# Interference stage of a tower kernel: a Newton step for all four lengths, half of the folding on VectorE, the third sum begun ahead of a negation

## The chip, the cores and the metric

One of the eight NeuronCores of a Trainium2 chip. The metric is the device time of one execution in microseconds (us), taken as the median of several executions. The profile shows one execution of its own; it is read against that execution's own time. Engines: TensorE (PE, with PEld for its weight loads), VectorE (DVE), ScalarE (ACT), GpSimd (POOL) and the SyncE queue (SP), which here issues most of the transfers.

## The reference, cut to what matters

1024 tokens pass two encoders and an attention over four states. What follows is the stage that this case is about. `R` and `I` are real and imaginary parts of four states `n` of 512 values for each token.

```python
R = einsum('bnd,ned->bne', attn_r, int_Wr) - einsum('bnd,ned->bne', attn_i, int_Wi)
I = einsum('bnd,ned->bne', attn_r, int_Wi) + einsum('bnd,ned->bne', attn_i, int_Wr)
phase = arctan2(I_i * R_j - R_i * I_j, R_i * R_j + I_i * I_j)     # for every pair i, j of states
f = cos(phase) * strength[..., None]
sup_r = einsum('bijd,bjd->bd', f, R)
sup_i = einsum('bijd,bjd->bd', f, I)
norm = sqrt(sum(sup_r ** 2 + sup_i ** 2) + 1e-08)
```

Then `sup / norm` goes through the measuring matrices, an amplitude, a layer norm, a GELU and three top layers (the tail). The kernel never forms a phase: the cosine of a phase between two states is the dot product of their unit vectors, so it needs `1 / sqrt(R^2 + I^2)` for each of the four states, and that length again to weigh the states in the sum.

## The kernel before, in words

All of it stands in `phase_states`. The tokens are eight tiles `t` of 128. The program of every engine is written out by hand and runs in its own order; engines meet in semaphores only. Tiles 0, 1 and 7 (LAST) are written out on VectorE and 2 to 6 are a hardware loop; on ScalarE the loop holds tiles 1 to 6.

For one tile:

- **PE** (`vectors(t, n)`, L52 to L54): 48 matmuls of 128x512 for each state `n`, results in banks `2n` (real) and `2n+1` (imaginary). It may overwrite the banks of state `n` once the unit vector of the tile before has been read out of them (`unit`). Its left operands `s_axng` are loaded into two buffers by SP (`load`, L787), and ScalarE makes the negated copies (`negate`, L994).
- **ACT**: `squares(t, n)` (L1003, L1004) puts the squares of both banks into `sqr` and `sqi`, which have two slots, shared by states 0/2 and 1/3. `magnitude` makes a mask `zero` (L1012) and the length `mag` (L1013, Sqrt). `seed` (L1017) overwrites `sqi` with a first guess of 1/length for states 2 and 3. `begin(t, 0, j)` (L1032) starts the weights `inv` from the dot product `p` that VectorE has just made. `length` and `scale` (L1042 to L1048) normalise the folded sum of the tile before. Functions of different tables need an ACT_TABLE_LOAD between them.
- **DVE** (class `Tile`): `add_squares(t, n)` (L1423) for states 0 and 1, written into the middle and the end of the tile before; `invert(n)` (L1333), a hardware reciprocal of 128x512 for states 0 and 1; `unit_vector(n)` (L1350); `add_23` (L1337); `pair(0, 1)` (L1355 to L1363); `refine` (L1341, L1343), one Newton step from the guess, for states 2 and 3 together; unit vectors 2 and 3; then the pairs 02, 03, 12, 13, 23, each four instructions with one or two `weigh` (L1372) and some `rescale` (L1378); last `product` (L1417), 128x4096, which multiplies all four vectors by their weights.
- **POOL** (`fold`, L872, L875): adds vectors 0 to 2 and 1 to 3 (two instructions of 128x1024), then 2 to 3 into `sup`. Beside it stands, on VectorE, the next tile's work.

ScalarE's order in a tile is squares 0, magnitude 0, negate(t, 3), squares 1, magnitude 1, negate(t+1, 0), squares 2 and 3, magnitude 2 and 3, seed, negate(t+1, 1), begin 1 (twice), length, begin 2, negate(t+1, 2), scale, begin 3. In the last tile it also splits weight pieces into high and low parts (`pieces`, L956; on VectorE L1284) and works for the tail (`sup_high`, L1078; on VectorE `sup_low`, L1451, L1453).

Of the kernel before, what the change touches and what calls it, by code (L numbers as in the profile page):

```python
# [10 lines left out]
ALU = mybir.AluOpType  # L11
# [512 lines left out]
def phase_states(nc, g):  # L524
# [13 lines left out]
    STEPS = 2 + 1 + 6 + 2 * 6 + 3 + sum(WEIGHED.values())  # L538
    W_MR, W_MI, W_POST, W_T1, W_T2 = 0, KD, 2 * KD, 3 * KD, 4 * KD
    with s.ctx:  # L540
# [327 lines left out]
        def _(pool):  # L868
            def fold(t):
                pool.wait_ge(weighed, t + 1)  # L870
                for n in range(2):
                    pool.tensor_tensor(cs[:, :, n + 2, :], cs[:, :, n, :], cs[:, :, n + 2, :], ALU.add).then_inc(folded, 1)  # L872
                pool.wait_ge(folded, t * 3 + 2)
                pool.wait_ge(stored, t * 16)
                pool.tensor_tensor(sup[:, :, :], cs[:, :, 2, :], cs[:, :, 3, :], ALU.add).then_inc(folded, 1)  # L875
# [11 lines left out]
            with pool.Fori(1, TT) as t:  # L887
                fold(t)

        @block.scalar  # L890
        def _(act):
# [114 lines left out]
            def magnitude(t, n0, n1):  # L1006
                n = slice(n0, n1)
                m = slice(n0 % 2, n0 % 2 + n1 - n0)
                act.wait_ge(summed, t * 3 + (min(n0, 2) + 1))
                if not zeroth(t):  # L1010
                    act.wait_ge(rescaled, t * 3 - (2 - min(n0, 2)))
                act.activation(zero[:, n, :], sqi[:, m, :], ACT.Relu, scale=-1.0 / LEAST, bias=k01[:, 1:2])  # L1012
                act.activation(mag[:, n, :], sqi[:, m, :], ACT.Sqrt, bias=k01[:, 0:1]).then_inc(mag_done, 1)  # L1013

            def seed(t):
                act.wait_ge(mag_done, t * 3 + 3)
                act.activation(sqi[:, :, :], sqi[:, :, :], ACT.Abs_reciprocal_sqrt, bias=k01[:, 0:1]).then_inc(seeded, 1)  # L1017
# [32 lines left out]
            def body(t, first):  # L1050
                squares(t, 0)
                magnitude(t, 0, 1)
                negate(t, 3)
                squares(t, 1)
                magnitude(t, 1, 2)
# [3 lines left out]
                magnitude(t, 2, 4)  # L1059
                seed(t)  # L1060
# [39 lines left out]
            def gelu(t):  # L1100
# [3 lines left out]
                else:  # L1104
                    act.wait_ge(newton, TT)
# [47 lines left out]
            magnitude(t, 0, 1)  # L1153
            negate(t, 3)
            squares(t, 1)
            magnitude(t, 1, 2)
# [5 lines left out]
            magnitude(t, 2, 4)  # L1162
            seed(t)
# [35 lines left out]
        def _(dve):  # L1199
# [119 lines left out]
            class Tile:  # L1319
# [9 lines left out]
                def invert(self, n):  # L1329
                    dve.wait_ge(mag_done, self.t * 3 + (n + 1))  # L1330
                    if not self.first and n == 0:
                        dve.wait_ge(weighed, self.t)
                    self.link(dve.reciprocal(inv[:, n, :], mag[:, n, :]))  # L1333

                def add_23(self):
                    dve.wait_ge(squared, self.t * 8 + 8)
                    dve.tensor_tensor(sqi[:, :, :], sqr[:, :, :], sqi[:, :, :], ALU.add).then_inc(summed, 1)  # L1337

                def refine(self):
                    dve.wait_ge(seeded, self.t + 1)  # L1340
                    self.link(dve.scalar_tensor_tensor(out=sqr[:, :, :], in0=mag[:, 2:4, :], scalar=-1.0, in1=sqi[:, :, :],  # L1341
                                                       op0=ALU.mult, op1=ALU.mult))
# [10 lines left out]
                def pair(self, i, j):  # L1353
                    t, p = self.t, p_of(i, j)
# [596 lines left out]
```

## Time and profile before

| what | us |
|---|---|
| median of 3 executions | 3120.39 (3120.31 to 3123.47) |
| the profiled execution, whole | 3116.82 |
| its span, first to last instruction | 3115.2 |
| first unit-vector work on VectorE of this stage to the end of tile 6 | 2559.1 to 2914.4 |
| last tile with the head of the tail | 2914.4 to about 2979 |
| the rest of the tail | about 2979 to 3115.2 |

How to read the profile: a timeline row gives the start in us, the duration, the engine, the line of the kernel, output<-input, and in brackets the idle time ahead of it with what ended it. Instructions of one engine overlap a little (the next starts some 0.08 us before the end shown), so that steps on a path are counted from start to start. The granted clock PEclk is a share of 2.4 GHz; 0.5 is the other level, 1.2 GHz.

### The profile page before, as it was taken

What the parts mean: (1) busy time and instruction counts of PE and PEld (TensorE: products, weight loads), DVE (VectorE), ACT (ScalarE), POOL (GpSimd) and SP (SyncE); (2) the same over time, 40 slices, a digit from 0 to 9 for tenths busy, and PEclk for the clock granted to TensorE, in tenths of its full rate; (3) what the DMA queues carried; (4) which work ended last, traced back from release to release, by engine and by line L of the source; (5) the groups of instructions that cost most, each with busy time, mean ns of one, the idle gap of its engine ahead of it and who ended that gap; (6) DMA issues with size and microseconds to landing.
All of it is one profiled execution on the core that took longest, in us unless ns stands there. A gap on an engine that the chain in (4) does not pass through costs nothing. (4 is left out here: it accounts for less than half of the span.)

```text
span 3115.2 us, 43855 instructions
## 1 busy us (share of the span) xinstructions
PE 2981.3 (96%) x15808; PEld 2582.6 (83%) x15808; DVE 1571.7 (50%) x2819; ACT 1111.3 (36%) x1873; POOL 233.0 (7%) x241
## 2 busy tenths in 40 slices
PE   8999999999699999999979999999999989999798
PEld 7888888888588877888879999999999977777686
DVE  3222222212531125221257767667667659999973
ACT  3111111111331114211235555545555554454553
POOL 1000000000110111110000000000000001212100
PEclk9999999999899999999989999999999999999899
DMA  5222222221442334332432232231231373433410
GB/s 203 75 77 74 74 77 74 64 60 61 152 146 77 101 98 139 106 104 76 152 120 55 69 93 54 80 81 54 84 78 54 101 183 81 108 94 88 147 40 11
DMA packets 364353, 285.48 MB, mean 92 GB/s; under 512 B 280193, under 2 KB 280321, under 8 KB 364161
## 3 DMA queue, kind: packets, MB, share of 16 engines
q1 hardware_dynamic: 341632, 206.97, 23.6%
q0 software_dynamic: 22656, 77.67, 7.2%
q8 instruction: 38, 0.62, 0.1%
q14 instruction: 27, 0.21, 0.0%
HBM read 194.40 MB, written 90.18 MB: 91 GB/s over the span
## 5 line engine op out<-in xcount | busy, mean ns | idle before, releaser
L52 PE MATMUL banks<-a_whi,g_hi 128*128 128x512 f32 x1152 | 449.0, 390 | 9.6 <-DVE a_wlo L185 9.6
L53 PE MATMUL banks<-a_wlo,g_hi 128*128 128x512 f32 x1152 | 448.8, 390 | 0.0
L54 PE MATMUL banks<-a_whi,g_lo 128*128 128x512 f32 x1152 | 448.6, 389 | 0.0
L52 PE MATMUL banks<-g_hi,b_whi 128*128 128x512 f32 x1024 | 400.6, 391 | 1.2 <-issue 1.2
L53 PE MATMUL banks<-g_lo,b_whi 128*128 128x512 f32 x1024 | 399.0, 390 | 0.0
L54 PE MATMUL banks<-g_hi,b_wlo 128*128 128x512 f32 x1024 | 398.8, 389 | 0.0
L185 DVE TENSOR_TENSOR a_wlo<-a_wraw,a_whi 128x512 fp32r<-128x512 f32 x144 | 99.6, 692 | 569.2 <-ACT a_whi L171 569.2
L171 ACT ACTIVATE a_whi<-a_wraw 128x512 fp32r<-128x512 f32 x144 | 91.0, 632 | 660.2 <-PE banks L54 660.2
L52 PE MATMUL banks<-t_sx,g_hi 128*128 128x256 f32 x1024 | 294.2, 287 | 17.7 <-DMA t_sx<-s_scr 17.7
L396 DVE TENSOR_TENSOR b_wlo<-b_wraw,b_whi 128x512 fp32r<-128x512 f32 x128 | 88.2, 690 | 433.3 <-ACT b_whi L341 433.1
L53 PE MATMUL banks<-t_sx,g_hi 128*128 128x256 f32 x1024 | 291.0, 284 | 0.0
L54 PE MATMUL banks<-t_sx,g_lo 128*128 128x256 f32 x1024 | 290.9, 284 | 0.0
L1206 DVE TENSOR_SCALAR t_ks<-banks,cols 64x256 f32<-64x256 f32 x512 | 236.5, 482 | 80.5 <-PE banks L54 73.3
L52 PEld LDWEIGHTS banks<-a_whi,g_hi 128*128 128x128 f32 x1152 | 216.6, 188 | 54.6 <-issue 9.5
L53 PEld LDWEIGHTS banks<-a_wlo,g_hi 128*128 128x128 f32 x1152 | 216.7, 188 | 45.1
L54 PEld LDWEIGHTS banks<-a_whi,g_lo 128*128 128x128 f32 x1152 | 216.6, 188 | 44.9
L341 ACT ACTIVATE b_whi<-b_wraw 128x512 fp32r<-128x512 f32 x128 | 80.3, 629 | 446.8 <-PE banks L54 446.1
L52 PE MATMUL banks<-g_hi,s_axng 128*128 128x512 f32 x512 | 205.6, 402 | 26.0 <-DVE s_cs L1350 23.4
L52 PEld LDWEIGHTS banks<-g_hi,b_whi 128*128 128x128 f32 x1024 | 192.7, 188 | 40.6 <-issue 1.4
L54 PEld LDWEIGHTS banks<-g_hi,b_wlo 128*128 128x128 f32 x1024 | 192.7, 188 | 40.3
L53 PEld LDWEIGHTS banks<-g_lo,b_whi 128*128 128x128 f32 x1024 | 192.7, 188 | 39.8
L52 PEld LDWEIGHTS banks<-t_sx,g_hi 128*128 128x128 f32 x1024 | 197.9, 193 | 18.4 <-issue 14.6
(158 smaller groups left out, 5567.0 us busy)
## 6 DMA issues: line engine op xcount, KB each, us to landing
a_wraw<-w_first SPq DMA_DIRECT2D x144, 256.0 KB, 2.6
b_wraw<-w_second SPq DMA_DIRECT2D x128, 256.0 KB, 2.6
t_sx<-s_scr SPq DMA_DIRECT2D x64, 512.0 KB, 4.1
a_scr<-t_at SPq DMA_DIRECT2D x256, 128.0 KB, 1.9
s_axng<-a_scr SPq DMA_DIRECT2D x64, 512.0 KB, 5.3
g_wraw<-w_pieces SPq DMA_DIRECT2D x82, 256.0 KB, 4.5
h_scr<-a_hst POOLq DMA_DIRECT2D x72, 256.0 KB, 2.7
b_hl<-h_scr POOLq DMA_DIRECT2D x16, 1024.0 KB, 5.9
```

Source lines behind the costliest of these rows:

```text
L52: mm(out, ahi, bhi, start=first, stop=False)
L53: mm(out, ahi, blo, start=False, stop=False)
L54: return mm(out, alo, bhi, start=False, stop=last)
L171: act.activation(whi[:, k % SPL, :], wraw[:, k % RAW, :], ACT.Copy).then_inc(w_hi, 1)
L185: dve.tensor_tensor(wlo[:, k % SPL, :], wraw[:, k % RAW, :], whi[:, k % SPL, :].bitcast(F32), ALU.subtract).then_inc(w_split, 1)
L341: act.activation(whi[:, j % SPL, :, :].rearrange("p a n -> p (a n)"), wraw[:, j % RAW, :], ACT.Copy).then_inc(w_hi, 1)
L396: dve.tensor_tensor(wlo[:, j % SPL, :, :].rearrange("p a n -> p (a n)"), wraw[:, j % RAW, :], whi[:, j % SPL, :, :].bitcast(F32).rearrange ...
L1206: ins = dve.tensor_scalar(ks[half(at_half), m % 2, h, part, :], b_k[half(h), m % 2, e * C:(e + 1) * C], bcol(M_K + e, m, half(h)), float(s ...
```

## The change

Four edits, all in this stage:

1. `invert` goes. All four lengths take the guess and Newton step: `lengths(t, h)` on ScalarE for the states of half `h` (0 and 1, or 2 and 3) computes the guess into `sqr`, then the length, then the mask; `refine(h)` on VectorE does the two instructions into `inv`.
2. Since the guess of half 0 now lies in `sqr`, `squares(t, 2)` and `squares(t, 3)` wait for `refine(0)`. The two half-size sums of squares become one of 128x1024, `add_squares(0)` just ahead of `product`; `add_23` becomes `add_squares(1)` and stands behind both unit vectors 0 and 1.
3. The two POOL additions into vectors 2 and 3 become one VectorE addition of 128x2048 behind `product`. POOL keeps the last addition, and waits for `refine(0)` of the next tile before it starts.
4. On ScalarE `negate(t+1, 2)` moves from ahead of `scale` and the third `begin` to behind them.

```diff
@@ POOL, fold
             def fold(t):
-                pool.wait_ge(weighed, t + 1)
-                for n in range(2):
-                    pool.tensor_tensor(cs[:, :, n + 2, :], cs[:, :, n, :], cs[:, :, n + 2, :], ALU.add).then_inc(folded, 1)
-                pool.wait_ge(folded, t * 3 + 2)
+                pool.wait_ge(folded, t * 2 + 1)
+                if not isinstance(t, int) or t < LAST:
+                    pool.wait_ge(newton, t * 2 + 3)
                 pool.wait_ge(stored, t * 16)
                 pool.tensor_tensor(sup[:, :, :], cs[:, :, 2, :], cs[:, :, 3, :], ALU.add).then_inc(folded, 1)
@@ ACT
             def squares(t, n):
                 act.wait_ge(multiplied, t * 8 + (2 * n + 2))
                 if n >= 2:
-                    act.wait_ge(mag_done, t * 3 + (n - 1))
+                    act.wait_ge(mag_done, t * 4 + 2)
+                    act.wait_ge(newton, t * 2 + 1)
                 elif not zeroth(t):
-                    act.wait_ge(newton, t)
+                    act.wait_ge(mag_done, t * 4)
+                    act.wait_ge(newton, t * 2)
...
-            def magnitude(t, n0, n1):
...
-            def seed(t):
...
+            def lengths(t, h):
+                n = slice(2 * h, 2 * h + 2)
+                act.wait_ge(summed, t * 2 + (h + 1))
+                act.activation(sqr[:, :, :], sqi[:, :, :], ACT.Abs_reciprocal_sqrt, bias=k01[:, 0:1]).then_inc(seeded, 1)
                 if not zeroth(t):
+                    act.wait_ge(rescaled, t * 3 - (1 - h))
+                act.activation(mag[:, n, :], sqi[:, :, :], ACT.Sqrt, bias=k01[:, 0:1]).then_inc(mag_done, 1)
+                act.activation(zero[:, n, :], sqi[:, :, :], ACT.Relu, scale=-1.0 / LEAST, bias=k01[:, 1:2]).then_inc(mag_done, 1)
...
             def body(t, first):
                 squares(t, 0)
-                magnitude(t, 0, 1)
                 negate(t, 3)
                 squares(t, 1)
-                magnitude(t, 1, 2)
+                lengths(t, 0)
                 negate(t + 1, 0)
                 squares(t, 2)
                 squares(t, 3)
-                magnitude(t, 2, 4)
-                seed(t)
+                lengths(t, 1)
...
                 begin(t, 0, 2)
-                negate(t + 1, 2)
                 if not first:
                     scale(t - 1)
                 begin(t, 0, 3)
+                negate(t + 1, 2)
@@ DVE, class Tile
+                def refine(self, h):
+                    n = slice(2 * h, 2 * h + 2)
+                    dve.wait_ge(seeded, self.t * 2 + (h + 1))
+                    dve.wait_ge(mag_done, self.t * 4 + (2 * h + 1))
...
+                    self.link(dve.scalar_tensor_tensor(out=inv[:, n, :], in0=mag[:, n, :], scalar=-1.0, in1=sqr[:, :, :],
                                                        op0=ALU.mult, op1=ALU.mult))
...
+                    dve.scalar_tensor_tensor(out=inv[:, n, :], in0=inv[:, n, :], scalar=2.0, in1=sqr[:, :, :],
                                              op0=ALU.add, op1=ALU.mult).then_inc(newton, 1)
...
                 def units(self):
-                    self.invert(0)
+                    self.refine(0)
                     self.unit_vector(0)
-                    self.add_23()
-                    self.invert(1)
                     self.unit_vector(1)
+                    self.add_squares(1)
...
                                       ALU.mult).then_inc(weighed, 1)
+                    dve.wait_ge(weighed, self.t + 1)
+                    dve.tensor_tensor(cs[:, :, 2:4, :], cs[:, :, 0:2, :], cs[:, :, 2:4, :], ALU.add).then_inc(folded, 1)
...
                 tile.pairs_12()
-                add_squares(t + 1, 0)
                 tile.pairs_13()
                 tile.pairs_23()
-                add_squares(t + 1, 1)
+                Tile(t + 1, False).add_squares(0)
                 tile.product()
```

Where this moves instructions, in the steady loop. REGISTER_ALU and ISA rows are small steps of the sequencer that compute a semaphore value. First VectorE, the head of a tile (loop of tiles 2 to 6); before:

```order
L1333 RECIPROCAL s_inv<-s_mag 128x512 [waits s_weighed,s_mag_done]
L1327 ISA
L1349 REGISTER_ALU [waits s_chain]
L1350 TENSOR_TENSOR s_cs<-banks,s_inv 128x2x512 [waits s_folded]
L1336 ISA
L1337 TENSOR_TENSOR s_sqi<-s_sqr,s_sqi 128x1024 [waits s_squared]
L1330 REGISTER_ALU
L1333 RECIPROCAL s_inv<-s_mag 128x512 [waits s_mag_done]
L1327 REGISTER_ALU
L1349 REGISTER_ALU [waits s_chain]
L1350 TENSOR_TENSOR s_cs<-banks,s_inv 128x2x512 [waits s_folded]
L1355 TENSOR_TENSOR s_zz<-s_zero 128x512
```

and with the change:

```order
L1331 ISA [waits s_seeded]
L1334 SCALAR_TENSOR_TENSOR s_inv<-s_mag,s_sqr 128x1024 [waits s_weighed,s_mag_done]
L1322 ISA
L1336 SCALAR_TENSOR_TENSOR s_inv<-s_inv,s_sqr 128x1024 [waits s_chain]
L1342 REGISTER_ALU [waits s_newton]
L1343 TENSOR_TENSOR s_cs<-banks,s_inv 128x2x512 [waits s_folded]
L1343 TENSOR_TENSOR s_cs<-banks,s_inv 128x2x512
L1325 ISA
L1326 TENSOR_TENSOR s_sqi<-s_sqr,s_sqi 128x1024 [waits s_squared]
L1349 REGISTER_ALU
L1350 TENSOR_TENSOR s_zz<-s_zero 128x512 [waits s_mag_done]
```

Two reciprocals have given way to two Newton instructions of double width, and the sum of squares of states 2 and 3 has moved from between the unit vectors to behind them.

Second ScalarE, from the squares of state 2 to the copy of the strengths; before:

```order
L1003 ACTIVATE s_sqr<-banks 128x512 [waits s_mag_done,s_multiplied]
L1004 ACTIVATE s_sqi<-banks 128x512
L998 REGISTER_ALU
L1003 ACTIVATE s_sqr<-banks 128x512 [waits s_mag_done,s_multiplied]
L1004 ACTIVATE s_sqi<-banks 128x512
L1009 REGISTER_ALU
L1012 ACTIVATE s_zero<-s_sqi,g_k 128x1024 [waits s_rescaled,s_summed]
L1013 ACTIVATE s_mag<-s_sqi,g_k 128x1024
L1017 ACT_TABLE_LOAD
L1017 ACTIVATE s_sqi<-s_sqi,g_k 128x1024 [waits s_mag_done]
```

and with the change:

```order
L1005 ACTIVATE s_sqr<-banks 128x512 [waits s_newton,s_mag_done]
L1006 ACTIVATE s_sqi<-banks 128x512
L998 REGISTER_ALU
L1005 ACTIVATE s_sqr<-banks 128x512 [waits s_newton,s_mag_done,s_multiplied]
L1006 ACTIVATE s_sqi<-banks 128x512
L1010 REGISTER_ALU
L1011 ACT_TABLE_LOAD
L1011 ACTIVATE s_sqr<-s_sqi,g_k 128x1024 [waits s_summed]
L1014 ACT_TABLE_LOAD
L1014 ACTIVATE s_mag<-s_sqi,g_k 128x1024 [waits s_rescaled]
L1015 ACTIVATE s_zero<-s_sqi,g_k 128x1024
```

The guess comes first, with a table load ahead of the instruction that waits for the sum, a second table load follows it, and the squares wait for VectorE's Newton step.

Third GpSimd, its loop over the tiles; before:

```order
L872 TENSOR_TENSOR s_cs<-s_cs 128x2x512 [waits s_weighed]
L872 TENSOR_TENSOR s_cs<-s_cs 128x2x512
L873 ISA
L874 REGISTER_ALU [waits s_folded]
L875 TENSOR_TENSOR s_sup<-s_cs 128x1024 [waits s_stored]
L887 REGISTER_ALU
```

and with the change:

```order
L872 REGISTER_ALU [waits s_folded]
L873 REGISTER_ALU [waits s_newton]
L874 TENSOR_TENSOR s_sup<-s_cs 128x1024 [waits s_stored]
L886 REGISTER_ALU
L886 COMPARE_AND_BRANCH
```

One of three additions is left on GpSimd, behind a wait for the next tile's Newton step.

## Rows read from the trace of the kernel before

**Rows 1.** By stretch: busy us (count) of PE, PEld, DVE, ACT, POOL; PEclk; DMA share; GB/s.
```profile
2700.00:2750.00 50.00, 45.94 (x192) 37.48 (x191) 47.56 (x50) 25.51 (x37) 7.93 (x3) 0.93 0.39 94
...
2622.00:2628.00 6.00, 5.43 (x13) 4.32 (x14) 5.96 (x4) 4.30 (x4) 3.80 (x2) 0.52 0.05 11
```

**Rows 2.** PE in order of time: the first matmul of tile 2's product.
```profile
2622.57 0.80 PE L52 MATMUL banks<-g_hi,s_axng 128*128 128x512 f32 x1 [6.16 <-DVE s_cs L1350]
```

**Rows 3.** VectorE in order of time, tile 2, from its start to the next.
```profile
2666.92 3.35 DVE L1333 RECIPROCAL s_inv<-s_mag 128x512 f32<-128x512 f32 x1
...
2677.28 0.41 DVE L1355 TENSOR_TENSOR s_zz<-s_zero 128x512 bf16<-128x512 bf16 x1
...
2680.70 1.22 DVE L1341 SCALAR_TENSOR_TENSOR s_sqr<-s_mag,s_sqi 128x1024 f32<-128x1024 f32 x1
...
2683.22 2.36 DVE L1350 TENSOR_TENSOR s_cs<-banks,s_inv 128x1024 f32<-128x1024 f32 x2
2685.49 0.42 DVE L1355 TENSOR_TENSOR s_zz<-s_zero 128x512 bf16<-128x512 bf16 x1
...
2711.30 0.68 DVE L1423 TENSOR_TENSOR s_sqi<-s_sqr,s_sqi 128x512 f32<-128x512 f32 x1
2711.90 4.42 DVE L1417 TENSOR_TENSOR s_cs<-s_cs,s_inv 128x4096 f32<-128x4096 f32 x1
2716.42 3.35 DVE L1333 RECIPROCAL s_inv<-s_mag 128x512 f32<-128x512 f32 x1
```

**Rows 4.** VectorE in order of time, tiles 0 and 1 and tile 7.
```profile
2574.04 1.23 DVE L1337 TENSOR_TENSOR s_sqi<-s_sqr,s_sqi 128x1024 f32<-128x1024 f32 x1 [10.34 <-ACT s_sqi L1004]
...
2582.87 1.23 DVE L1341 SCALAR_TENSOR_TENSOR s_sqr<-s_mag,s_sqi 128x1024 f32<-128x1024 f32 x1
...
2617.90 3.35 DVE L1333 RECIPROCAL s_inv<-s_mag 128x512 f32<-128x512 f32 x1
...
2636.04 0.42 DVE L1355 TENSOR_TENSOR s_zz<-s_zero 128x512 bf16<-128x512 bf16 x1
...
2645.66 1.23 DVE L1361 TENSOR_TENSOR s_tt<-s_cs 128x1024 f32<-128x1024 f32 x1 [0.63 <-ACT s_inv L1032]
...
2914.45 3.35 DVE L1333 RECIPROCAL s_inv<-s_mag 128x512 f32<-128x512 f32 x1
...
2930.65 0.68 DVE L1453 SCALAR_TENSOR_TENSOR g_lo<-banks,g_hi 128x512 fp32r<-128x512 f32 x1
```

**Rows 5.** ScalarE in order of time, tile 2.
```profile
2668.82 0.60 ACT L1003 ACTIVATE s_sqr<-banks 128x512 f32<-128x512 f32 x1 [2.24 <-PE banks L54]
2669.32 0.59 ACT L1004 ACTIVATE s_sqi<-banks 128x512 f32<-128x512 f32 x1
...
2673.84 1.13 ACT L1013 ACTIVATE s_mag<-s_sqi,g_k 128x1024 f32<-128x1024 f32 x1
2674.99 1.28 ACT L1017 ACT_TABLE_LOAD   x1
2676.29 1.15 ACT L1017 ACTIVATE s_sqi<-s_sqi,g_k 128x1024 f32<-128x1024 f32 x1
```

**Rows 6.** ScalarE in order of time, tail: a table load ahead of a wait.
```profile
2977.84 1.28 ACT L1088 ACT_TABLE_LOAD   x1
2985.88 0.63 ACT L1088 ACTIVATE s_ef<-s_ef 128x512 f32<-128x512 f32 x1 [6.75 <-DVE s_ef L1461]
```

**Rows 7.** POOL and VectorE in order of time, 2993 to 3002.
```profile
2993.51 4.76 POOL L872 TENSOR_TENSOR s_cs<-s_cs 128x1024 f32<-128x1024 f32 x2 [71.11 <-DVE s_cs L1417]
2998.43 2.65 POOL L875 TENSOR_TENSOR s_sup<-s_cs 128x1024 f32<-128x1024 f32 x1 [0.16 <-POOL s_cs L872]
...
2996.19 2.63 DVE L1483 TENSOR_TENSOR g_lo<-s_sqi,g_hi 128x512 fp32r<-128x512 f32 x1 [0.36 <-ACT g_hi L1113]
...
2999.34 2.28 DVE L1461 TENSOR_TENSOR s_ef<-s_ef 128x512 f32<-128x512 f32 x1
```

**Rows 8.** The tile s_axng: its loads, issue to landing.
```profile
DMA to landing us min/median/max: 3.8/5.3/8.1
```

More of the change, by code:

```diff
@@ L537, in phase_states @@
     WEIGHED = {(0, 1): 0, (0, 2): 1, (0, 3): 1, (1, 2): 2, (1, 3): 2, (2, 3): 2}
-    STEPS = 2 + 1 + 6 + 2 * 6 + 3 + sum(WEIGHED.values())
+    STEPS = 2 + 6 + 2 * 6 + 3 + sum(WEIGHED.values())
     W_MR, W_MI, W_POST, W_T1, W_T2 = 0, KD, 2 * KD, 3 * KD, 4 * KD
@@ L886, in _ @@
             fold(0)
-            with pool.Fori(1, TT) as t:
+            with pool.Fori(1, LAST) as t:
                 fold(t)
+            fold(LAST)
         @block.scalar
@@ L1161, in _ @@
             sup_high(0)
-            magnitude(t, 2, 4)
-            seed(t)
+            lengths(t, 1)
             strengths(t)
@@ L1327, in link, with add_squares @@
                     dve.wait_ge(chain, self.t * STEPS + self.done)
-                def invert(self, n):
-                    dve.wait_ge(mag_done, self.t * 3 + (n + 1))
-                    if not self.first and n == 0:
-                        dve.wait_ge(weighed, self.t)
[L1333 to L1341, printed above, removed]
+                def add_squares(self, h):
+                    dve.wait_ge(squared, self.t * 8 + (4 * h + 4))
+                    dve.tensor_tensor(sqi[:, :, :], sqr[:, :, :], sqi[:, :, :], ALU.add).then_inc(summed, 1)
+                def refine(self, h):
+                    n = slice(2 * h, 2 * h + 2)
+                    dve.wait_ge(seeded, self.t * 2 + (h + 1))
+                    dve.wait_ge(mag_done, self.t * 4 + (2 * h + 1))
+                    if h == 0 and not self.first:
+                        dve.wait_ge(weighed, self.t)
+                    self.link(dve.scalar_tensor_tensor(out=inv[:, n, :], in0=mag[:, n, :], scalar=-1.0, in1=sqr[:, :, :],
                                                        op0=ALU.mult, op1=ALU.mult))
-                    dve.scalar_tensor_tensor(out=inv[:, 2:4, :], in0=sqr[:, :, :], scalar=2.0, in1=sqi[:, :, :],
+                    dve.scalar_tensor_tensor(out=inv[:, n, :], in0=inv[:, n, :], scalar=2.0, in1=sqr[:, :, :],
                                              op0=ALU.add, op1=ALU.mult).then_inc(newton, 1)
-                    dve.wait_ge(newton, self.t + 1)
+                    dve.wait_ge(newton, self.t * 2 + (h + 1))
                 def unit_vector(self, n):
-                    if not self.first and n < 3:
-                        dve.wait_ge(folded, self.t * 3 - (2 - n))
+                    if not self.first and n in (0, 2):
+                        dve.wait_ge(folded, self.t * 2 - (1 - n // 2))
                     dve.tensor_tensor(cs[:, :, n, :], g.ps[:, 2 * n:2 * n + 2, :],
@@ L1354, in pair @@
                     t, p = self.t, p_of(i, j)
+                    if i == 0 and j < 3:
+                        dve.wait_ge(mag_done, t * 4 + 2 * j)
                     self.link(dve.tensor_tensor(zz[:, :], zero[:, i, :], zero[:, j, :], ALU.add))
@@ L1418, in product @@
                                       ALU.mult).then_inc(weighed, 1)
+                    dve.wait_ge(weighed, self.t + 1)
+                    dve.tensor_tensor(cs[:, :, 2:4, :], cs[:, :, 0:2, :], cs[:, :, 2:4, :], ALU.add).then_inc(folded, 1)
                     assert self.done == STEPS
-            def add_squares(t, n):
-                dve.wait_ge(squared, t * 8 + (2 * n + 2))
-                dve.tensor_tensor(sqi[:, n, :], sqr[:, n, :], sqi[:, n, :], ALU.add).then_inc(summed, 1)
             def body(t, first):
@@ L1427, in body @@
                 if first:
-                    add_squares(t, 0)
-                    add_squares(t, 1)
+                    tile.add_squares(0)
                 tile.units()
                 tile.pair(0, 1)
-                tile.refine()
+                tile.refine(1)
                 tile.unit_vector(2)
@@ L1534, in _ @@
             tile.pair(0, 1)
-            tile.refine()
+            tile.refine(1)
             tile.unit_vector(2)
```

18 lines of the change are left out of this document (5 added, 13 removed).

## The prediction

> **What bounds the kernel now.** I began with busy time by stretch. In a steady 50 us of this stage VectorE is busy for 47.56 and TensorE for 45.94, part of it at a clock of 0.93 [rows 1]: two engines are nearly full, and the busy shares don't say which one sets the pace. TensorE in order of time does. It stands still for 6.16 us until VectorE's first unit vector of tile 1 is there [rows 2], and in the 6 us from 2622 on its granted clock is 0.52 [rows 1], close to the lower level of 1.2 GHz. From 2622.57 its four states take until the squares of state 3 can start at 2668.82 [rows 2, 5]: 46.2 us. VectorE goes from the first reciprocal of tile 2 at 2666.92 to that of tile 3 at 2716.42 [rows 3]: 49.50 us, with no idle stretch that names another engine. So VectorE sets a period of 49.5, and TensorE waits for it by some 3 us in each. What leaves VectorE's path shortens the period until 46.2 is met, and what only leaves GpSimd brings nothing by itself. The reader should see in rows 3 that steps are counted from start to start, since durations overlap.
>
> I call the first VectorE instruction behind `product` S. Tile 1 has S = 2617.90, tile 2 2666.92, tile 3 2716.42, tile 7 2914.45 [rows 3, 4].
>
> **The change, part by part: VectorE's own work in a steady tile.**
> - Two reciprocals go. From the first to the mask sum (L1355) it is 2677.28 - 2666.92 = 10.36 [rows 3]. Two unit vectors are 2685.49 - 2683.22 = 2.27 of that, the sum of squares 1.23 less an overlap of 0.08, 1.15. The rest, 6.94, is two reciprocals with their links, 3.35 each in the row.
> - The Newton step of half 0 comes in: 2683.22 - 2680.70 = 2.52 [rows 3].
> - The folding of 128x2048 comes in. Rows have 128x1024 at 1.23 and 128x4096 at 4.42 [rows 3, 4], so 2048 is 1.23 + 3.19/3 = 2.29, less the 0.08 of overlap, 2.2 on the path.
> - Two sums of 512, 0.60 each by 2711.90 - 2711.30 [rows 3], plus 0.1 for a sequencer step beside one of them, become one of 1024, about 1.15. That saves 0.15.
>
> Alone this is 6.94 - 2.52 - 2.2 + 0.15 = 2.4 us a tile.
>
> **What the new order of the engines costs.** S to the end of refine(0) is 2.2 + 2.5 = 4.7. Call that e. Is the guess there in time? ScalarE may begin it at the start of `product`, 4.52 before S; guess 1.15, load 1.28, root 1.14 [rows 5] end about 3.7 after that start, 0.8 before S, and refine(0) begins 2.2 behind S. 3 us of cover, so no cost.
>
> At e ScalarE may square states 2 and 3. Four such instructions follow each other by 0.50 or a little less [rows 5] and take 2.1, to e+2.2. VectorE does unit vectors 0 and 1 meanwhile, 2.27 for two, and is at add_squares(1) at e+2.3. That matches. But GpSimd's last addition starts at e too, and takes 2.65 when alone [rows 7]. In rows 7 a VectorE addition with both inputs in SBUF of 128x512 takes 2.63 instead of the 0.68 of such a one in rows 3, and another 2.28, and both end 0.54 behind the end of the GpSimd instruction beside them (2998.27 and 3001.08). add_squares(1) is of that kind; the unit vectors read a bank and are not. It is held until e+2.75 and ends at about e+3.85. Cost 0.4; bounds 0 (no hold) and 0.7 (GpSimd starts late behind its two sequencer steps).
>
> From there two chains run to refine(1). VectorE needs pair(0, 1), 2680.70 - 2677.28 = 3.42 [rows 3]: e+7.2. ScalarE's first table load stands ahead of the waiting instruction and waits for nothing; that such a load does run early is shown by one that starts at 2977.84 with its ACTIVATE 6.75 us idle behind it [rows 6]. It runs from e+2.2 to e+3.5, beside the sum. Then guess 1.15, load 1.28, root 1.14 [rows 5], with 0.1 of signalling: e+7.6. So VectorE waits 0.4. Before, it had a reciprocal and a unit vector more as cover, and no wait.
>
> refine(1) to the mask sum of pair(0, 2) is unchanged, 2685.49 - 2680.70 = 4.79 [rows 3]. That point lies at S+4.7+7.6+4.8 = S+17.1 instead of 2685.49 - 2666.92 = 18.57: gain 1.5. With the sums' 0.15 and up to 0.1 from the third `begin`, a steady tile gains 1.75 and the period is 47.75.
>
> **Other engines in that period.** TensorE starts its next tile at S+6.0 instead of S+4.7, and ends it 46.2 later, 4.4 behind the next S. The squares of state 3 can't start before 5.7 behind S: 1.3 us of slack. Loads: the one behind TensorE's last state is issued at S+4.4 and lands 5.3 later, at most 8.1 [rows 8], by S+12.5; ScalarE comes to its negation at about S+14. negate(t+1, 2), which moves behind the third `begin`, is done by S+27, and TensorE needs it at S+6.0+24.5 = S+30.5. Nothing costed. The last addition on POOL is also moved past a wait, but its reader, `length`, comes at S+17, so it is hidden. One table load per tile ahead of `length` goes, where ScalarE was idle: nothing.
>
> The Trainium skill, page "ScalarE: Activation LUTs", section "What ACT_TABLE_LOAD costs", speaks against the change: a switch of table costs about 2.66 us in all, the load and a drain of some 1.38. Here the guess starts 0.02 behind the load's end [rows 5], so no drain is seen; by the page's figure the load between guess and root would cost an estimated 1.4 more in each of seven tiles, and the sum below would be 10 smaller. Rival B is what the kernel would do then.
>
> **The sum.**
> - Tile 0: no folding, no GpSimd. The sum of states 2 and 3 starts at 2574.04 [rows 4] and ends 1.2 later at 2575.25; guess, load, root and signals, 3.75, lead to refine(1) at 2579.0 instead of 2582.87 [rows 4]. Gain 3.9, and 0.05 by the sums.
> - Tile 1: the mask sum stood at 2636.04 - 2617.90 = S+18.14 [rows 4], since code outside the loop has fewer sequencer steps; now S+17.1. Gain 1.05. It also had 0.63 idle for the third `begin`, held by a negation [rows 4]; the move ends that. With the sums 1.7.
> - Tiles 2 to 6: 5 x 1.75 = 8.8.
> - Tile 7: from S to the end of the low half for the tail took 2930.65 + 0.68 - 2914.45 = 16.9 [rows 4]. Now 4.7; then ScalarE squares, splits four pieces at about 0.52 and squares again, to e+4.3; sum 1.15; VectorE's eight pieces and sup_low, 6.6: S+16.8. Gain 0.1.
> - Tail: the last folding adds 2.2 to VectorE behind the last `product`, but ends GpSimd's two long instructions, which had held two additions by 1.9 and 1.6 [rows 7]. I put 0.3 of loss, with bounds -1 and +2.
>
> Gain 3.95 + 1.7 + 8.8 + 0.1 - 0.3 = 14.3. Profiled execution: 3116.8 - 14.3 = 3102.5. It lay 3.6 below the median of the runs, so the median becomes 3120.4 - 14.3 = **3106.1**.
>
> **Rivals.**
> A, no hold and no wait: GpSimd and VectorE don't meet, ScalarE is as quick as the pair. Then the 0.8 of each of seven tiles comes back in part; with all of it 5 us more, 3101. Rows 7 speak against it.
> B, a table load more on the path: the one ahead of the guess isn't hidden, or the one behind it takes as much again. 1.28 [rows 5] x 7 tiles = 9 off the gain: 3115. The gap of 0.02 in rows 5 and the early load in rows 6 speak against it. (The page named above would make it 3116.)
> C, the gain doesn't reach the end: TensorE's tail waits for a transfer or for VectorE's longer last tile, and more than half is lost, 3114 to 3120. That the whole chain from tile 7 hangs on VectorE's S speaks against it.
> D, slower: TensorE takes over. After a pause its clock is near half for about 6 us [rows 1], which costs about 3 of the 46.2. The new order ties VectorE's head to TensorE's end through the squares of state 3, with 1.3 us of slack. If the slow clock stays for 12 us more in each tile, a tile on TensorE takes 52.2; the squares then come 4.7 late and the period is about 52, 3120 + 6 x 2.5 = 3135. It decides from 47.5 us of TensorE time a tile, and costs against the kernel before from 49.5. For it: the clock does fall after each pause. Against: the pause gets shorter.
>
> **How the numbers follow.** Forecast, with small errors of its terms: 0.78, 3103 to 3110. A 0.07, B 0.06, C 0.06, D 0.03. A change of 0.2%, 6.2 us, is about what a measurement can tell from none; the line lies at 3120.4 - 6.2 = 3114.2. The forecast and A are faster by more: 0.85. B and most of C lie within: 0.11. D and a rest are slower: 0.04. The range from 3101 to 3112 takes in A and leaves out B, most of C and D, 0.15; its upper end has room for a hold of 0.7 in each tile and the tail's bound of 2.
>
> **What would show it.** Period of VectorE in tiles 2 to 6: 47.75; 47.0 means A, over 49 means B or D. refine(0) without idle ahead of it. add_squares(1) at 1.5 to 1.7 us and ending 0.5 to 1.1 behind GpSimd's. Idle of 0.4 ahead of refine(1), named after ScalarE's `mag`; 1.7 means B. No idle of VectorE named after the third `begin`. TensorE's pause down from about 3 to 1.5 us. S of tile 7 at 2900. The forecast is wrong if the two chains behind e are not as long as the rows say, or if a load lands more than 2 us later than any of before.

## The result, and the profile after

| | before | after |
|---|---|---|
| median of the runs, us | 3123.21 (5 runs, 3120.31 to 3124.16) | 3106.63 (5 runs, 3103.98 to 3107.61) |
| ratio | | 0.9948, 95% interval 0.9936 to 0.9960 |
| profiled execution, whole / span, us | 3116.82 / 3115.2 | 3107.61 / 3105.5 |
| period of VectorE, tiles 2 to 6, us | 49.50 | 47.46 |

The kernel is 0.5% faster. A second series of both kernels gave 3121.23 (15 runs) and 3107.06 (5 runs), ratio 0.9960 (0.9947 to 0.9974). The forecast was 3106.1, with a gain of 14.3; the two series show gains of 16.6 and 14.2.

VectorE in order of time, from tile 2's S to tile 3's. L1414 is the folding, L1334 and L1336 a Newton step, L1343 unit vectors, L1326 a sum of squares, L1350 a mask sum:
```profile
2665.13 2.29 DVE L1414 TENSOR_TENSOR s_cs<-s_cs 128x2048 f32<-128x2048 f32 x1
2667.34 1.22 DVE L1334 SCALAR_TENSOR_TENSOR s_inv<-s_mag,s_sqr 128x1024 f32<-128x1024 f32 x1
2668.59 1.22 DVE L1336 SCALAR_TENSOR_TENSOR s_inv<-s_inv,s_sqr 128x1024 f32<-128x1024 f32 x1
2669.94 2.36 DVE L1343 TENSOR_TENSOR s_cs<-banks,s_inv 128x1024 f32<-128x1024 f32 x2
2672.21 1.24 DVE L1326 TENSOR_TENSOR s_sqi<-s_sqr,s_sqi 128x1024 f32<-128x1024 f32 x1
2673.37 0.41 DVE L1350 TENSOR_TENSOR s_zz<-s_zero 128x512 bf16<-128x512 bf16 x1
...
2677.13 1.23 DVE L1334 SCALAR_TENSOR_TENSOR s_inv<-s_mag,s_sqr 128x1024 f32<-128x1024 f32 x1 [0.48 <-ACT s_mag L1014]
...
2681.93 0.41 DVE L1350 TENSOR_TENSOR s_zz<-s_zero 128x512 bf16<-128x512 bf16 x1
...
2712.60 2.29 DVE L1414 TENSOR_TENSOR s_cs<-s_cs 128x2048 f32<-128x2048 f32 x1
```
Read it against [rows 3]. From S to the mask sum of pair (0, 2) it is 2681.93 - 2665.13 = 16.80, where 18.57 stood. From there to the next S it is 30.67 instead of 30.93. The one idle stretch that names another engine is the 0.48 ahead of refine(1).

GpSimd and ScalarE in the same tile, and TensorE's first matmul of tile 3's product:
```profile
2669.98 2.38 POOL L874 TENSOR_TENSOR s_sup<-s_cs 128x1024 f32<-128x1024 f32 x1 [44.65 <-DVE s_inv L1336]
...
2669.91 0.60 ACT L1005 ACTIVATE s_sqr<-banks 128x512 f32<-128x512 f32 x1 [3.40 <-DVE s_inv L1336]
...
2672.00 1.28 ACT L1011 ACT_TABLE_LOAD   x1
2673.48 1.16 ACT L1011 ACTIVATE s_sqr<-s_sqi,g_k 128x1024 f32<-128x1024 f32 x1 [0.20 <-DVE s_sqi L1326]
2674.65 1.28 ACT L1014 ACT_TABLE_LOAD   x1
2675.95 1.15 ACT L1014 ACTIVATE s_mag<-s_sqi,g_k 128x1024 f32<-128x1024 f32 x1
...
2671.22 0.50 PE L52 MATMUL banks<-g_hi,s_axng 128*128 128x512 f32 x1 [1.62 <-DVE s_cs L1343]
```
GpSimd's addition waits for refine(0) and ends at 2672.36, as VectorE turns from the unit vectors (one operand in a bank) to the sum of squares (both in SBUF). The first table load runs beside that sum. The second stands on the path, at 1.28 with a gap of 0.02.

The stretches that answer to [rows 1], two tiles of after (busy us of PE, PEld, DVE, ACT, POOL; PEclk; DMA share; GB/s):
```profile
2712.56:2760.01 47.45, 43.80 (x181) 35.70 (x181) 44.96 (x49) 25.91 (x36) 2.36 (x1) 0.93 0.41 99
2760.01:2807.48 47.47, 46.62 (x206) 38.29 (x205) 44.96 (x49) 25.91 (x36) 2.38 (x1) 1.00 0.42 100
```
TensorE's clock is 0.93 in one and 1.00 in the other, and VectorE's period is the same in both: VectorE still sets the pace. TensorE's first matmul in each of the two:
```profile
2718.68 0.80 PE L52 MATMUL banks<-g_hi,s_axng 128*128 128x512 f32 x1 [3.65 <-DVE s_cs L1343]
```
```profile
2766.13 0.50 PE L52 MATMUL banks<-g_hi,s_axng 128*128 128x512 f32 x1 [0.85 <-DVE s_cs L1343]
```
Its pause ahead of a tile is 1.62, 3.65, 0.85, 3.65 and 2.15 us in the steady tiles of after, 2.4 on average, so the 1.62 above is not typical.

### The profile page after: what moved, and what is told of

Read it like the earlier page. It is cut to its first block and busy times, and to the rows that moved or that the text cites. A ratio compares the mean times of both kernels' runs of the same rounds, so it can differ in the third digit from the quotient of the medians.

```text
span 3105.5 us, 43835 instructions
## 1 busy us (share of the span) xinstructions
PE 2977.1 (96%) x15808; PEld 2578.7 (83%) x15808; DVE 1551.4 (50%) x2819; ACT 1124.1 (36%) x1869; POOL 189.8 (6%) x225
```

## The experiments

S stands for the first VectorE instruction behind `product`, as in the prediction, and a period is S to S in the steady tiles. In the expectations plane `n` is the banks or the vector of state `n`, and a turn is a tile. Differences between kernels of some 2 us can't be read from medians here, since single runs of one kernel lie up to 10 apart; the periods repeat within about 0.05.

**One part of the change alone: the third sum.**
```
  begin(t, 0, 2)
- negate(t + 1, 2)
  if not first:
      scale(t - 1)
  begin(t, 0, 3)
+ negate(t + 1, 2)
```


> The kernel before with one edit: ScalarE begins the third weighted sum ahead of the negation of plane 2 instead of behind it. Nothing else is changed. My theory: in the kernel before the wait of VectorE for that sum shows in tile 1 only (0.63 us), so the edit alone brings 0.6 to 1 us, 3122.4 us against 3123.2. Rival: the wait stood in every tile under another name and the edit brings 7 times 0.6, 3119.0 us.

Measured: 3121.05, ratio 0.9998 (0.9989 to 1.0007), period 49.51. Tile 1 took 48.41 instead of 49.02, as my theory has it. But the kernel before, profiled a second time unchanged, took 48.47 there:

> The kernel before, unchanged, for a second profile. My theory: the period of the tiles is 49.50 us again and the tail's intervals 20.0, while the point at which the turns start moves by a few us (2617.5 to 2623.7 in the profiles so far, of whatever kernel), and the end takes 21 or 22.5 us by the clock that is granted there. Rival: the kernel before starts its turns earlier and ends faster in every execution, so a part of the change's gain is lost in those two places.

Its one time was 3119.34. ScalarE in its tile 1, and then in the first profile of before:
```profile
2642.59 1.15 ACT L994 ACTIVATE s_axng<-s_axng 128x512 fp32r<-128x512 f32 x2 [1.95 <-DMA s_axng<-a_scr]
```
```profile
2642.63 1.15 ACT L994 ACTIVATE s_axng<-s_axng 128x512 fp32r<-128x512 f32 x2 [2.48 <-DMA s_axng<-a_scr]
```
The negation waits for a transfer, which lands at the same time from the start of the span, while the second profile's tile began 0.49 later. So VectorE's wait of 0.63 [rows 4] belonged to that one execution; the second profile has none. The moved sum takes away the chance of it; I can't show a gain from it.

**The other part alone: the Newton step, folding on GpSimd.**
```
- pool.wait_ge(folded, t * 2 + 1)
- if not isinstance(t, int) or t < LAST:
-     pool.wait_ge(newton, t * 2 + 3)
+ pool.wait_ge(weighed, t + 1)
+ for n in range(2):
+     pool.tensor_tensor(cs[:, :, n + 2, :], cs[:, :, n, :], cs[:, :, n + 2, :], ALU.add).then_inc(folded, 1)
+ pool.wait_ge(folded, t * 3 + 2)
```


> The kernel after with the folding given back to GpSimd: its two additions behind the product as before, then the third without the wait for the Newton step. So this is the Newton step and the moved sum without the move of the folding. My theory (VectorE's operations on two SBUF operands and GpSimd's additions exclude each other): the two GpSimd additions of 2.35 and the two halves of refine(0) of 1.24 take turns, so the first unit vector starts 7.2 us behind the product and not 4.8 as in the kernel after; 2.4 us a tile over 7 tiles is 16.8 us more, 3123.4 us (3120 to 3125), that is no faster than the kernel before. Rival (the two engines run side by side): the unit vectors wait only for the additions, the tile gets 1.2 us shorter than after, TensorE's slack lets it through, and the time is 3098 us.

Measured: 3121.09, ratio 0.9999 (0.9990 to 1.0008), period 49.60. VectorE's Newton step (first two rows) and GpSimd:
```profile
2670.01 3.45 DVE L1335 SCALAR_TENSOR_TENSOR s_inv<-s_mag,s_sqr 128x1024 f32<-128x1024 f32 x1
2673.50 3.29 DVE L1337 SCALAR_TENSOR_TENSOR s_inv<-s_inv,s_sqr 128x1024 f32<-128x1024 f32 x1
...
2669.98 5.72 POOL L872 TENSOR_TENSOR s_cs<-s_cs 128x1024 f32<-128x1024 f32 x2 [40.06 <-DVE s_cs L1412]
2675.88 3.14 POOL L875 TENSOR_TENSOR s_sup<-s_cs 128x1024 f32<-128x1024 f32 x1 [0.17 <-POOL s_cs L872]
```
Each half takes about as long as itself and a GpSimd addition together, 1.22 + 2.3. The two engines take turns and don't share. The Newton step alone, then, gains nothing.

**Folding alone, reciprocals kept.** The kernel before, with
```
+ dve.wait_ge(weighed, self.t + 1)
+ dve.tensor_tensor(cs[:, :, 2:4, :], cs[:, :, 0:2, :], cs[:, :, 2:4, :], ALU.add).then_inc(folded, 1)
```
behind `product` and one addition left to GpSimd.

> The kernel before with one edit: the folding of the four planes to two is VectorE's, behind the product, and GpSimd adds the last two. Reciprocals, their order and the third sum stay as in the kernel before. My theory: VectorE sets the period, the folding costs it 2.3 us a tile, and what it saves is small, since the reciprocals read one operand and were not held by GpSimd: 7 times 2.2 is 15.4 us more, 3138.6 us. Rival (the holds of GpSimd's additions cost the kernel before as much as the folding costs here): 3123 us.

Measured: 3137.9, ratio 1.0050 (1.0036 to 1.0064), period 51.56, that is 2.06 more a tile. GpSimd's addition, beside a reciprocal:
```profile
2674.65 3.34 DVE L1330 RECIPROCAL s_inv<-s_mag 128x512 f32<-128x512 f32 x1
...
2674.91 2.34 POOL L872 TENSOR_TENSOR s_sup<-s_cs 128x1024 f32<-128x1024 f32 x1 [48.57 <-DVE s_cs L1417]
```
Neither is held: 3.34 and 2.34 are what each takes at best in these profiles. In the kernel before, GpSimd's first two additions of tile 2 stand beside the reciprocal of [rows 3]:
```profile
2666.89 4.69 POOL L872 TENSOR_TENSOR s_cs<-s_cs 128x1024 f32<-128x1024 f32 x2 [41.02 <-DVE s_cs L1417]
```
So there the reciprocal covered them at 2.34 each, and taking it away, as the experiment above did, uncovers them.

**Everything but GpSimd's wait.**
```
  pool.wait_ge(folded, t * 2 + 1)
- if not isinstance(t, int) or t < LAST:
-     pool.wait_ge(newton, t * 2 + 3)
```


> The kernel after with one edit: GpSimd's addition no longer waits for the Newton step, only for VectorE's folding. My theory: it starts as the folding ends, beside refine(0), holds one of its halves by 2.38 us in every tile, and the time is 7 times 2.3, 16 us more: 3122.7 us. If GpSimd is the one that is held, its row gets longer by 1.2 to 2.5 and the time stays within 3106 to 3110. Rival (no exclusion, the wait is idle care): 3106.6 us and the two halves of refine(0) keep their 1.24 us back to back.

Measured: 3120.02, ratio 0.9994 (0.9985 to 1.0003), period 49.50, 2.04 more than after. VectorE's two halves, and GpSimd:
```profile
2668.71 1.22 DVE L1332 SCALAR_TENSOR_TENSOR s_inv<-s_mag,s_sqr 128x1024 f32<-128x1024 f32 x1
2669.96 3.30 DVE L1334 SCALAR_TENSOR_TENSOR s_inv<-s_inv,s_sqr 128x1024 f32<-128x1024 f32 x1
...
2668.96 3.21 POOL L872 TENSOR_TENSOR s_sup<-s_cs 128x1024 f32<-128x1024 f32 x1 [45.78 <-DVE s_cs L1412]
```
GpSimd starts while the first half runs, and its row is 0.83 longer than 2.38; then the second half is held by 2.08. Two lines of waiting carry nearly the whole gain of the change, 2.04 in each of seven tiles. The rows fit the Trainium skill, page "SBUF — State Buffer", section "SBUF: two separate sides", by which one of the two has the shared pair of ports for its whole instruction and the other one waits.

**A table load more on the path.**
```
  act.activation(sqr[:, :, :], sqi[:, :, :], ACT.Abs_reciprocal_sqrt, bias=k01[:, 0:1]).then_inc(seeded, 1)
+ if h == 1:
+     act.activation(nrm[:, 3:4], k01[:, 1:2], ACT.Exp)
```


> The kernel after with one instruction more on ScalarE in each tile: an Exp of one column, its result read by nobody, between the reciprocal square root and the square root of lengths 2 and 3. It needs a table of its own, so one more table load stands on ScalarE's path from the sum of the squares to mag, which refine(1) already waits for (0.48 us of idle in a steady tile). My theory: the price is the load's own 1.28 us and about 0.25 for the small Exp, all of it on VectorE's path in 8 tiles: 12 us more, 3118.5 us. Rival 1 (the path from ScalarE had slack left elsewhere, or the load runs early): 3106.6 us. Rival 2 (a load costs more than its row, by about as much again): 20 us more, 3127 us. The Trainium skill, page 'ScalarE: Activation LUTs', section 'What ACT_TABLE_LOAD costs', would put it near rival 2.

Measured: 3117.7 (10 runs, widely spread, 3112.86 to 3122.82), ratio 0.9990 (0.9981 to 0.9999), period 48.95, 1.49 more than after. ScalarE, and VectorE's refine(1):
```profile
2675.42 1.28 ACT L1013 ACT_TABLE_LOAD   x1
2676.72 0.20 ACT L1013 ACTIVATE s_nrm<-g_k 128x1 f32<-128x1 f32 x1
2676.92 1.28 ACT L1016 ACT_TABLE_LOAD   x1
...
2679.41 1.22 DVE L1336 SCALAR_TENSOR_TENSOR s_inv<-s_mag,s_sqr 128x1024 f32<-128x1024 f32 x1 [1.98 <-ACT s_mag L1016]
```
A load costs its row and nothing behind it: from load to load it is 1.50, and the wait grew from 0.48 to 1.98. So that wait of the kernel after is real, and a load costs 1.3 and not twice that. The 2.66 us a switch of the Trainium skill, page "ScalarE: Activation LUTs", section "What ACT_TABLE_LOAD costs", is not met: rival 2 would need a period of some 50.1.

**The last folding, and the same kernel again.**
```
+ if isinstance(t, int) and t == LAST:
+     pool.wait_ge(weighed, t + 1)
+     pool.tensor_tensor(cs[:, :, 2:4, :], cs[:, :, 0:2, :], cs[:, :, 2:4, :], ALU.add).then_inc(folded, 1)
```
and no folding on VectorE in that tile.

> The kernel after, with the folding of the last tile only given to GpSimd (one addition of 128x2048 elements and one of 128x1024); the seven tiles before keep it on VectorE. My theory: the three kernels so far with VectorE's folding in the last tile show one interval of 20.8 us in the tail where the three with GpSimd's folding show 20.0, so here the interval is back at 20.0 and the time 0.8 us less, 3105.8 us. Rival: the interval stays at 20.8, because it comes from the earlier start of the tail and not from the folding, and the time is that of the kernel after; or GpSimd holds a later operation of VectorE by more than 0.8 us and the time is 1 to 2 us above it.

> The kernel after, unchanged, for a second profile and more times beside the others on one chip. If the start-up (4.16 us later up to the first sum of squares than in the profile of before) belongs to the one execution, it is different here; if the change makes it, it stays. The same for the end of the tail: 22.6 us from the last GELU to the end in the profile of after, 21.1 in that of before. My theory: both belong to the execution, and the median is within 1.5 us of 3106.6.

Measured: 3107.27 and 3107.06. The tail has eight GELU steps. In the second profile of after it is 20.89 from the second to the third, with the last folding on GpSimd 20.02. (This is the interval that the expectations speak of.) In all fourteen profiles it is 20.8 to 20.9 where VectorE does the last folding, and 20.0 where GpSimd does. From tile 7's S to the end it is 201.6 instead of 202.6 and 203.1 in the two profiles of after. VectorE behind the last `product` in after, with L1441 the first instruction of `sup_low`:
```profile
2981.35 2.29 DVE L1414 TENSOR_TENSOR s_cs<-s_cs 128x2048 f32<-128x2048 f32 x1
2983.56 1.28 DVE L1441 TENSOR_TENSOR g_lo<-banks,g_hi 128x512 fp32r<-128x512 f32 x2
```
TensorE's waits in after from 2975 to 3010 (us in total, times, longest):
```profile
PE banks L52 <- DVE g_lo L1455: 0.6, 1, 0.6
```
With the last folding on GpSimd, VectorE:
```profile
2978.99 4.42 DVE L1414 TENSOR_TENSOR s_cs<-s_cs,s_inv 128x4096 f32<-128x4096 f32 x1
2983.33 1.28 DVE L1447 TENSOR_TENSOR g_lo<-banks,g_hi 128x512 fp32r<-128x512 f32 x2
```
Here `sup_low` follows `product` at once, and TensorE waits for nothing in that stretch. That the 0.8 arrives at the end is shown by the trace alone; the medians can't tell it. What the second profile of after says of the start and of the last microseconds stands further down.

**Beyond the change: the 0.48, and the waits behind the mask sum.** Two ideas to shorten VectorE's tile. The first splits the squares (and does add_squares(1) ahead of unit_vector(1), with GpSimd's addition in two halves, the second behind that sum):
```
+ act.wait_ge(mag_done, t * 4 + 2)
+ for n in (2, 3):
+     act.wait_ge(multiplied, t * 8 + (2 * n + 2))
+     act.activation(sqi[:, n % 2, :], g.ps[:, 2 * n + 1, :], ACT.Square).then_inc(squared, 1)
+ act.wait_ge(newton, t * 2 + 1)
+ for n in (2, 3):
+     act.activation(sqr[:, n % 2, :], g.ps[:, 2 * n, :], ACT.Square).then_inc(squared, 1)
```


> The kernel after, rearranged to take away the 0.48 us in which VectorE waits for mag ahead of refine(1): in the steady tiles ScalarE squares the imaginary parts of planes 2 and 3 before it waits for refine(0), VectorE adds the squares behind the first unit vector instead of the second, and GpSimd's addition is cut in two halves, the second behind that sum. Nothing is left out. My theory: the wait goes, the halves fit beside the two unit vectors, 0.3 to 0.48 us a tile over 7 tiles are 2 to 3.4 us, 3103.5 us. Rival: a half of GpSimd's addition is still running as the sum of the squares or the first zero-mask sum wants to start and holds it by about what was gained, and the time stays at 3106 to 3109 us.

Measured: 3108.95, ratio 0.9960 (0.9946 to 0.9974), period 47.40: a miss. In tile 2 the wait moved. ScalarE and VectorE:
```profile
2670.29 0.60 ACT L1015 ACTIVATE s_sqi<-banks 128x512 f32<-128x512 f32 x1 [2.70 <-PE banks L54]
...
2671.89 1.23 DVE L1337 TENSOR_TENSOR s_sqi<-s_sqr,s_sqi 128x1024 f32<-128x1024 f32 x1 [0.38 <-ACT s_sqr L1018]
```
State 3 is not out of TensorE earlier, 4.8 us behind S here. But that wait stands in tile 2 only. In tiles 3 to 6 the squares are in time, and what takes the gain is the other side of the recorded rival: the mask sum, both operands in SBUF, meets the second half of GpSimd's addition. VectorE and GpSimd, tile 3:
```profile
2721.58 0.59 DVE L1361 TENSOR_TENSOR s_zz<-s_zero 128x512 bf16<-128x512 bf16 x1
...
2720.60 1.29 POOL L877 TENSOR_TENSOR s_sup<-s_cs 128x512 f32<-128x512 f32 x1 [1.16 <-DVE s_sqi L1337]
```
It takes 0.59 instead of 0.41, the wait ahead of refine(1) is still 0.21, and from S to refine(1) it is 11.94, where after has 11.98. In tile 7 VectorE waits 3.02 for the squares instead of 1.89. So TensorE was not the bound in these tiles, though the next expectations read it so.

The second idea, alone and with the last folding on GpSimd:
```
- self.link(dve.tensor_tensor(zz[:, :], zero[:, i, :], zero[:, j, :], ALU.add))
+ dve.tensor_tensor(zz[:, :], zero[:, i, :], zero[:, j, :], ALU.add).then_inc(chain, 1)
+ self.done += 1
```


> The kernel after with one edit: behind the sum of two zero masks (zz) VectorE no longer waits for that sum to be done before it starts the product of the pair, which doesn't read it; the wait behind the product covers both. Nothing is left out. In a steady tile of the kernel after the six waits are 0.19 us each, 1.14 us. My theory: VectorE sets the period and TensorE still waits 1.6 us a tile, so nearly all of it arrives, except that of pair (0,1), which stands ahead of refine(1) and only makes its wait for mag longer: 5 times 0.19 is 0.95 us a tile, 7 tiles are 6.6 us, 3100.3 us, with TensorE's wait down to 0.6. Rival (in the kernel with the squares split a VectorE that was ready earlier gained 0.05 us a tile only, since plane 3 was not there: TensorE is the bound already): 0.1 us a tile, 3106 us.

> The kernel before this one (no wait behind zz) with the folding of the last tile only given to GpSimd. My theory: the two savings lie in different stretches and add up, 0.8 us less than without that folding, 3099.5 us, and the intervals of the tail are 20.0 us each. Rival: the shorter tiles put the tail's third interval elsewhere and the 0.8 is not there.

Measured: 3101.3 (5 runs, 3098.0 to 3101.73), ratio 0.9925 (0.9912 to 0.9939) against before, period 46.51, 0.95 less than after, as expected. The sum behind the 0.95 was not: counted from start to start, the product follows the mask sum 0.33 after it instead of 0.61 in three pairs and 0.46 in the other three, so a wait costs 0.28 or 0.12 and not 0.19 each. The one of pair (0, 1) gains nothing, since the wait for `mag` grew to 0.75, as it should. With the last folding on GpSimd the time is 3101.31 (0.9928, 0.9915 to 0.9942), the interval in the tail again 20.0, but the 0.8 is not to be seen in the medians. Both kernels beat the one after. The last run puts all three together:

> The kernel with no wait behind zz and GpSimd's folding of the last tile, and with the squares split, the sum of squares behind the first unit vector and GpSimd's addition cut in halves (the last tile keeps the order of the kernel after for its squares and unit vectors). Nothing is left out. Without the split VectorE waits 0.75 us a tile for mag ahead of refine(1), and TensorE stands still for 1.0 to 2.7 us a tile, so plane 3 is there when its imaginary part is to be squared. My theory: where the split gained only 0.05 us a tile in the longer tile, since plane 3 came late, it now gains 0.5 to 0.75 a tile, 7 tiles are 3.5 to 5 us, 3097 us, and the period is 45.9. Rival: as in the kernel with the split alone VectorE meets the squares and the zero mask instead, the period stays at 46.4 to 46.5 and the time at 3101 us.

Measured: 3102.34, ratio 0.9935 (0.9922 to 0.9949), a miss again. Its periods alternate, 47.54, 46.17, 47.17, 46.18 and, in tile 6, 48.29. VectorE in tile 2, a long one:
```profile
2672.53 1.23 DVE L1340 TENSOR_TENSOR s_sqi<-s_sqr,s_sqi 128x1024 f32<-128x1024 f32 x1 [1.29 <-ACT s_sqr L1021]
```
The first four periods as stretches (columns as above):
```profile
2665.16:2712.70 47.54, 47.13 (x209) 38.71 (x208) 44.69 (x49) 25.85 (x36) 2.59 (x2) 1.00 0.43 103
2712.70:2758.87 46.17, 42.45 (x181) 34.64 (x180) 44.61 (x49) 25.97 (x36) 2.56 (x2) 0.96 0.42 100
2758.87:2806.04 47.17, 46.41 (x205) 38.13 (x204) 44.68 (x48) 25.86 (x36) 2.57 (x2) 1.00 0.43 102
2806.04:2852.22 46.18, 42.82 (x178) 34.87 (x177) 44.62 (x48) 25.98 (x36) 2.57 (x2) 0.93 0.39 93
```
and TensorE's first matmul of two tiles in a row:
```profile
2718.83 0.63 PE L52 MATMUL banks<-g_hi,s_axng 128*128 128x512 f32 x1 [3.73 <-DVE s_cs L1357]
```
```profile
2764.99 0.50 PE L52 MATMUL banks<-g_hi,s_axng 128*128 128x512 f32 x1 [0.76 <-DVE s_cs L1357]
```
From 2718.83 to the pause of 0.76 TensorE works for 45.4 us, with a clock of 0.96 in the stretch of that tile; the tiles that follow a pause of 0.4 or 0.8 take it 43.8, at 1.00. So after a long pause it is late with state 3 for the next sum of squares; the next pause is then short, and it is early again. VectorE pays 1.29, 0.94 and 2.05 us in tiles 2, 4 and 6 and waits for no other engine in tiles 3 and 5. TensorE thus holds VectorE in every second tile, along the path of rival D, through the squares of state 3 and the clock behind a pause, and the mean period is 47.1 instead of 46.5. But it isn't busy throughout, and the 47.5 us a tile of rival D are met nowhere. That the lower clock makes the lateness is read from these tiles; no run tests it by itself.

## Why the prediction was right

| term | forecast, us | measured, us |
|---|---|---|
| S to the end of refine(0) | 4.7 | 4.81 |
| from there to refine(1), with its wait | 7.6 (0.4) | 7.19 (0.48) |
| refine(1) to the mask sum | 4.8 | 4.80 |
| rest of the tile, gain | 0.25 | 0.26 |
| period | 47.75 | 47.46 |
| tile 0, gain | 3.95 | 3.94 |
| tile 1, gain | 1.7 | 2.01 |
| S of tile 1 to S of tile 7, gain | 10.5 | 12.27 |
| tile 7 up to sup_low, gain | 0.1 | 0.08 |
| from there to the end | -0.3 | -2.43 |

All of it is from the two first profiles; the terms add up to 13.9, against the forecast's 14.3. Two of them were wrong and nearly cancel: the gain of tiles 1 to 6 was put 1.8 too low and that of the tail 2.1 too high. That the median came within 0.5 of 3106.1 is partly luck, for this reason and since the median of before went from 3120.39 to 3123.21 with two more runs. The profiled execution was to take 3102.5 and took 3107.6.

**The mechanism was right.** VectorE set the period. Without the folding on VectorE nothing is gained (3121.1), without GpSimd's wait next to nothing (3120.0), and the folding without the Newton step loses 16 us (3137.9). The folding's 2.29 was met to the digit. The tables were hidden or cheap as argued, so rival B had no ground: 1.3 a load.

**The hold was mis-sized.** The prediction priced GpSimd's addition at 2.65 "when alone" [rows 7] and let it hold add_squares(1) by 0.4. It takes 2.38, and ends as the unit vectors end; the sum of squares ran at 1.24. The 2.65 itself was the row of an instruction held by VectorE's, in the very rows that I cited for holds; the addition was not alone there, since VectorE's two-operand row beside it ends at 2998.82, 0.39 behind its start. The true term is 0 to 0.08, and the period 0.3 shorter for it. That is the half of rival A by which the two don't meet. Rows 7, set against it, show only what happens when they do: the engines exclude each other, and the wait for the Newton step keeps them apart.

**TensorE's 46.2 was no fixed time.** It was read in a tile that followed a pause of 6.16. From the first matmul to the next pause it is 43.8 us in after where the clock is 1.00 and 45.3 to 46.6 where it is 0.93 or 0.96 (2718.68 to 2766.13 less 0.85 is 46.6). So the pauses came down to 2.4 on average and not to 1.5, and there was more room under 47.46 than the prediction saw; the sum doesn't use the term.

**The tail was mis-sized**, by 2.1. 0.8 is the last folding, which stands ahead of `sup_low`; the prediction set it against the end of GpSimd's holds, but the kernel with the last folding on GpSimd has those holds again and loses nothing by them. The other 1.5 lies behind the start of the last GELU, 22.6 us to the end in after and 21.1 in before. TensorE's granted clock from 20 to 10 us before the end, in before, in its second profile, and in after:
```profile
3095.20:3105.20 10.00, 5.80 (x34) 4.94 (x35) 3.54 (x7) 2.12 (x5) 0.00 (x0) 1.00 0.05 2
```
```profile
3097.00:3107.00 10.00, 7.60 (x36) 6.33 (x37) 2.91 (x7) 0.60 (x1) 0.00 (x0) 0.83 0.04 0
```
```profile
3085.50:3095.50 10.00, 7.31 (x34) 6.00 (x35) 3.20 (x7) 0.65 (x2) 0.00 (x0) 0.83 0.04 0
```
Of the fourteen profiles of this study four have 1.00 there and take 20.8 to 21.3 us from the last GELU to the end; the other ten have 0.83 and 21.9 to 22.9. The kernel before is found on both sides, so this is no cost of the change as far as these profiles tell. What decides it stayed open. Without it the change's terms are 15.4.

**The third sum** was put at 0.63 in tile 1. That wait was real in the profile but not in the next one. Tile 1's gain against the second profile of before is 1.46.

**The start.** In after the first sum of squares of states 2 and 3 comes 4.16 later in the span than in before, 2578.20 against 2574.04. The first matmul of this stage is already 4.4 later (2529.1 and 2524.7), and no line ahead of it is touched. That accounts for the step from the 13.9 of the terms to the 9.7 by which the two spans differ. My theory that it belongs to the one execution was not borne out by the times: in the second profile of after the sum comes at 2578.10, in that of before at 2574.55. The place differs, though. At the first instruction of L193, an addition in the first stage near 95 us, the first profile of after is 3.8 behind before and the second only 0.8; it loses the rest later. And other kernels with the same code ahead of this stage begin it from 2525.7 to 2530.9. Whether the change has a part in it is open, and so is why both profiled executions of before (3116.82 and 3119.34) were faster than its medians, so that the profiles differ by 9 and 12 us and the medians by 14 to 17.

## What to carry to other kernels

Taking a long one-operand instruction off VectorE can uncover GpSimd's additions behind it; price the pair together, and start GpSimd's two-operand work, by a wait if need be, beside VectorE's operations that read a bank, if no short two-operand one stands among them. Take the duration of an instruction from a row beside which the other engine is idle or reads one operand, never from the row that shows the hold. Before trusting a wait that stands in one tile only, ask whether its other side is a transfer. And look at every steady tile before naming what took a gain: one tile showed a wait for TensorE that the next four don't have.

## What the runs showed of the hardware

- VectorE and GpSimd take turns by whole instructions when both operands are in SBUF: 3.45 and 3.29 instead of 1.22 on one side, 5.72 for two and 3.21 instead of 2.34 to 2.38 each on the other. A reciprocal (3.34 beside GpSimd's 2.34) or an operation with one operand in a bank (2.36 for two beside GpSimd's 2.38) is not held, and doesn't hold.
- A wait on VectorE for its own last instruction, where the next one doesn't need it, costs 0.12 to 0.28 from start to start behind a mask sum of 128x512; six of them a tile were 0.95 of the period, and 6 us of the kernel.
- TensorE's granted clock over a period is 0.93 to 0.96 in the tiles with a pause of 3.4 to 3.8 us, and 1.00 in those with one of 0.4 to 0.9 (after and the last kernel); at a pause of 2.7 both are found in one profile. Two engines that are nearly balanced can fall into a rhythm of two tiles by it, and a mean over both hides which one waits.
